# Two attentions: scores and row maxima two groups ahead, turned maxima one group ahead in mid-group

## The reference, cut to what matters

```python
def xattn(query, key, value):           # layer 0; layer 1 is the same with biases and no mask
    q, k, v = split_heads(query @ Wq.T), split_heads(key @ Wk.T), split_heads(value @ Wv.T)
    scores = einsum("bhqd,bhkd->bhqk", q, k) / sqrt(16)
    scores = where(causal | attention_mask, -inf, scores)
    attn = softmax(scores, axis=-1)
    return merge_heads(einsum("bhqk,bhkd->bhqd", attn, v)) @ Wout.T + b_out

x = x + xattn(layernorm(x), ctx, ctx)   # attention 0
x = x + moe_16_experts(layernorm(x))
x = x + xattn(layernorm(x), ctx, ctx)   # attention 1
x = x + moe_7_experts_and_a_shared(layernorm(x))
```

## Time and profile before

| what | us |
| --- | --- |
| runs of the kernel | 1264.04, 1265.51, 1271.85 |
| median | 1265.51 |
| span of the profiled execution | 1262.1 |
| its own time | not listed apart from the three runs |
| a middle batch of attention 0 / its groups | 24.3 / 4 |
| a middle batch of attention 1 / its groups | 23.5 / 4 |

### The profile page before, as it was taken

How to read it: one execution, slowest core, us unless ns; L and a number is a source line. 1 busy time by engine, 2 the same in 40 slices (tenths; PEclk the granted TensorE clock), 3 DMA queues, 4 the chain that set the end, 5 groups by cost and what they waited for, 6 DMA issues and landing times. The chain is left out here.

```text
span 1262.1 us, 25941 instructions
## 1 busy us (share of the span) xinstructions
PE 1123.7 (89%) x8539; PEld 974.6 (77%) x8539; DVE 690.8 (55%) x1558; ACT 595.9 (47%) x1211; POOL 360.7 (29%) x502
## 2 busy tenths in 40 slices
PE   5999998739999984888998679999999999999997
PEld 4788786329888873555665379999999999999996
DVE  4755666652222226676767655555556555555556
ACT  3566666313222222776787334444445444444432
POOL 6566650112222205776630145000000000000261
PEclk8899999859999996999999879999999999999999
DMA  7774461548999957568471221223232232232132
GB/s 182 175 180 120 129 179 37 193 159 292 332 330 325 314 207 163 111 136 146 89 125 24 100 89 59 79 63 112 72 103 76 87 109 87 86 100 73 50 97 80
DMA packets 88137, 172.56 MB, mean 137 GB/s; under 512 B 11251, under 2 KB 59949, under 8 KB 81792
## 3 DMA queue, kind: packets, MB, share of 16 engines
q1 hardware_dynamic: 71712, 136.15, 39.0%
q0 software_dynamic: 9584, 29.32, 7.9%
q10 hardware_dynamic: 6768, 6.16, 1.4%
HBM read 133.11 MB, written 39.20 MB: 137 GB/s over the span
## 5 line engine op out<-in xcount | busy, mean ns | idle before, releaser
L2136 PE MATMUL e_ps<-xT_e,wp_e 128*128 128x384 f32 (+1 forms) x1344 | 245.2, 331 | 4.0 <-DVE wp_e L2010 4.0
L2136 PEld LDWEIGHTS e_ps<-xT_e,wp_e 128*128 128x128 f32 x1344 | 221.7, 188 | 5.4 <-issue 4.1
L639 DVE TENSOR_REDUCE att_ps<-att_ps 128x2 f32<-128x512 f32 (+1 forms) x224 | 155.3, 697 | 103.5 <-PE att_ps L986 63.2
L1968 ACT ACTIVATE act_a_e<-e_ps 128x256 f32<-128x256 f32 (+2 forms) x176 | 77.8, 442 | 159.9 <-PE e_ps L2136 150.9
L2066 DVE TENSOR_TENSOR hid_e<-act_a_e,e_ps 128x256 f32<-128x256 f32 (+2 forms) x176 | 87.0, 494 | 116.6 <-ACT act_a_e L1968 102.4
L892 ACT ACTIVATE probs<-att_ps 128x384 f32<-128x384 f32 (+1 forms) x256 | 130.4, 546 | 41.4 <-PE att_ps L1018 29.0
L1972 ACT ACTIVATE hidp_e<-hid_e 128x256 fp32r<-128x256 f32 (+2 forms) x176 | 83.8, 476 | 127.3 <-DVE hid_e L2066 121.5
L2153 PE MATMUL e_ps<-wp_e,hidp_e 128*128 128x256 f32 (+1 forms) x1008 | 138.4, 282 | 2.9 <-DVE xres L2026 1.2
L2068 DVE TENSOR_TENSOR hidp_e<-hid_e,hidp_e 128x256 fp32r<-128x256 f32 (+2 forms) x176 | 87.8, 499 | 95.5 <-ACT hidp_e L1972 90.1
L2153 PEld LDWEIGHTS e_ps<-wp_e,hidp_e 128*128 128x128 f32 (+1 forms) x1008 | 130.7, 183 | 4.9 <-issue 4.1
L1608 ACT ACTIVATE hid_e<-e_ps,b_ahead 128x128 f32<-128x128 f32 x188 | 53.7, 368 | 139.9 <-PE e_ps L1713 129.2
(11 more groups left out here) (235 smaller groups left out, 1850.0 us busy)
## 6 DMA issues: line engine op xcount, KB each, us to landing
w_e<-in_W SPq DMA_DIRECT2D x47, 1024.0 KB
w_e<-in_W SPq DMA_DIRECT2D x57, 384.0 KB, 3.1
ks<-parts SPq DMA_DIRECT2D x96, 128.0 KB, 4.7
qs<-parts SPq DMA_DIRECT2D x96, 128.0 KB, 5.2
parts<-cut SPq DMA_DIRECT2D x30, 384.0 KB, 3.2
x_e<-rows SPq DMA_DIRECT2D x8, 768.0 KB, 5.6
done<-y_e ACTq DMA_DIRECT2D x47, 128.0 KB
rows<-zeros POOLq DMA_DIRECT2D x8, 736.5 KB, 6.6
```

The source lines that it names most:

```text
L639: dve.tensor_reduce(tops_at(at[3])[:, qt, x0:x0 + heads], src, AX.X, ALU.max).then_inc(reduced, 1)
L1968: act.activation(act_a[:, u % 2, 0:n], ps[:, AB + u % 2, 0:n], ACT.Silu).then_inc(silu_ready, 1)
L2136: last = pe.matmul(ps[:, bank + u % 2, 0:n], weights(lot, c, pw)[:, (b * DC + d) * P:(b * DC + d + 1) * P], xT[:, px, d, t0:t0 + n], start ...
```

## The change

Scores and maxima are computed two groups ahead instead of one (`after(after(at))` on TensorE and VectorE), the turn and the copy of the maxima one group ahead, in the middle of a group: after the second transposed score on TensorE, and after the second exponential on ScalarE. The values of the group before move behind the second transposed score as well, the turn of their output to the group's end. The row maxima are kept in a new SBUF tile `row_tops`, and their turned row in PSUM bank MB, so that the wait on the exponentials before the turn is dropped. A prologue computes the scores, maxima and copied row of the first groups.

```diff
--- before.py
+++ after.py
@@ -184,6 +184,7 @@
         qs, ks = sb("qs", [KT, 2, H, S], BF16), sb("ks", [KT, 2, H, S], BF16)
         stacks = (qs, ks)
         top_parts = sb("top_parts", [P, 2, TPB, 2, G], BF16)
+        row_tops = sb("row_tops", [P, 2, TPB, G])
         probs = sb("probs", [P, 2, G, TPB * S])
         v = sb("v", [P, 2, TPB, H, ROWS])
         o = sb("o", [P, 2, S])
@@ -304,9 +305,13 @@
 
             return bank + f if early(f) else XB
 
+        def turned_tops(lo, hi):
+
+            return ps[KS:KT, MB, lo:hi]
+
         def tops_at(g):
 
-            return ps[:, MB, (g % 2) * TPB * G:(g % 2 + 1) * TPB * G].rearrange("p (t x) -> p t x", t=TPB)
+            return row_tops[:, g % 2]
 
         def comes(n, kind):
 
@@ -695,13 +700,13 @@
                 gathered = ye is not None and normed_ahead(n)
                 for g in range(NG):
                     at = (n, j, r, g)
-                    more, started = not (last and g == NG - 1), not (first and g == 0)
+                    more, started = not (last and g >= NG - 2), not (first and g == 0)
                     for u in range(NU):
                         if g == 0 and u == 0 and gathered:
                             rows_back(dve, f)
                             dve.wait_ge(root_ready, f - 1)
                         if more:
-                            reduce(after(at), u)
+                            reduce(after(after(at)), u)
                         if g == 0 and gathered:
                             t, c = u % TPB, u // TPB
                             if u == TPB:
@@ -722,7 +727,7 @@
                         if g == 3 and u and not first and u <= TPB:
                             statistics(n - 1, u - 1)
                     if more:
-                        tops(after(at))
+                        tops(after(after(at)))
                     if started:
                         normalize(prior(at))
                     if g == 2 and first and ye is None:
@@ -787,11 +792,12 @@
                     dve.wait_ge(later_ready, 1)
                     close(dve, 0)
                 split(dve, 1, 1)
-            for u in range(NU):
-                reduce((0, 0, 0, 0), u)
-            tops((0, 0, 0, 0))
-            if ye is None:
-                split(dve, 1, 0)
+            for g in range(2):
+                for u in range(NU):
+                    reduce((0, 0, 0, g), u)
+                tops((0, 0, 0, g))
+                if ye is None and g == 0:
+                    split(dve, 1, 0)
             batches(dve, batch)
             normalize((B - 1, 1, None, NG - 1))
             residual(B - 1)
@@ -878,12 +884,6 @@
             def batch(n, j, r, first, last):
                 for g in range(NG):
                     at = (n, j, r, g)
-                    act.wait_ge(top_turned, ready(group(at)))
-                    act.activation(qs[KS:KT, j, g * G:(g + 1) * G, :], ps[KS:KT, TB, 0:S].unsqueeze(1).to_broadcast([2 * G, G, S]),
-                                   ACT.Copy).then_inc(row_ready, 1)
-                    if not (first and g == 0):
-                        take(prior(at))
-
                     act.wait_ge(valued, free(group(at)))
                     for x0 in range(G):
                         slot = g * G + x0
@@ -892,6 +892,18 @@
                         act.activation(probs[:, g % 2, x0, 0:WIDE], ps[:, TB + x0 % RING, 0:WIDE], ACT.Exp, scale=DK ** -0.5).then_inc(exped, 1)
                         if slot in H_SLOTS and fed(n):
                             norm_rows(n + FEED, j, H_SLOTS.index(slot))
+                        if x0 == 1:
+                            if not (first and g == 0):
+                                take(prior(at))
+                            if not (last and g == NG - 1):
+                                set_rows(after(at))
+
+            def set_rows(at):
+
+                n, j, r, g = at
+                act.wait_ge(top_turned, ready(group(at)))
+                act.activation(qs[KS:KT, j, g * G:(g + 1) * G, :], turned_tops(0, S).unsqueeze(1).to_broadcast([2 * G, G, S]),
+                               ACT.Copy).then_inc(row_ready, 1)
 
             def square_root(f, n, k):
 
@@ -924,6 +936,7 @@
                     take_values(f)
             if ye is None:
                 act.activation(warm[:], offset[:, 0:1], ACT.Exp)
+            set_rows((0, 0, 0, 0))
             batches(act, batch)
             take((B - 1, 1, None, NG - 1))
             take_all(B - 1)
@@ -992,9 +1005,8 @@
             def turn_tops(at):
                 n, j, r, g = at
                 pe.wait_ge(top_ready, ready(group(at)))
-                pe.wait_ge(exped, free(n * H + g * G))
                 for t in range(TPB):
-                    last = pe.matmul(ps[KS:KT, TB, t * P:(t + 1) * P], top_parts[:, g % 2, t].rearrange("p a g -> p (a g)"),
+                    last = pe.matmul(turned_tops(t * P, (t + 1) * P), top_parts[:, g % 2, t].rearrange("p a g -> p (a g)"),
                                      m["identb"][:], start=True, stop=True, tile_position=(0, KS))
                 last.then_inc(top_turned, 1)
 
@@ -1099,32 +1111,33 @@
             def batch(n, j, r, first, last):
                 for g in range(NG):
                     at = (n, j, r, g)
-                    more, started = not (last and g == NG - 1), not (first and g == 0)
+                    more, started = not (last and g >= NG - 2), not (first and g == 0)
 
                     def score_next(u):
                         if more and u < NU:
-                            score(after(at), u)
+                            score(after(after(at)), u)
 
                     if first and g == NG - 1 and ahead is None:
                         pe.wait_ge(wo_loaded, 16)
                     score_next(0)
-                    turn_tops(at)
-                    if started:
-                        value(prior(at))
-                    score_next(1)
                     scoreT(at, 0)
                     feed(n, j, r, g * G)
                     if ye is not None and first and g == 0:
                         pe.wait_ge(taken[0], FEED)
                     scoreT(at, 1)
+                    if started:
+                        value(prior(at))
+                    score_next(1)
+                    feed(n, j, r, g * G + 1)
+                    if not (last and g == NG - 1):
+                        turn_tops(after(at))
+                    scoreT(at, 2)
                     score_next(2)
-                    feed(n, j, r, g * G + 1)
+                    feed(n, j, r, g * G + 2)
+                    scoreT(at, 3)
+                    score_next(3)
                     if started:
                         turn_o(prior(at))
-                    scoreT(at, 2)
-                    score_next(3)
-                    feed(n, j, r, g * G + 2)
-                    scoreT(at, 3)
                     feed(n, j, r, g * G + 3)
 
             if constants:
@@ -1167,6 +1180,10 @@
                 pe.wait_ge(identb_ready, 1)
             for u in range(0 if ye is None else RING, NU):
                 score((0, 0, 0, 0), u)
+            score((0, 0, 0, 1), 0)
+            turn_tops((0, 0, 0, 0))
+            for u in range(1, NU):
+                score((0, 0, 0, 1), u)
             batches(pe, batch)
             ended = (B - 1, 1, None, NG - 1)
             value(ended)
```

## The result

The changed kernel takes 1323.93 us (median of 4 runs, 1319.71 to 1331.02), the kernel before 1268.13 (1264.04 to 1271.85): ratio 1.0443, interval 1.041 to 1.0477, so it is slower by some 56 us. The forecast was 1288.5 with a range to 1302: the sign is right, but the 23 us forecast are less than half of the 56, and the time lies outside the range. The profiled execution is the longest of the four (1331.02 us), that of before the shortest of its own (1264.04), so stage by stage the traces differ by 67 us and not by 56.

The account below looks back on a forecast made before the run. It took the stack's landing, asked for one group earlier, as the bound: +14.5 us in attention 0 and +8.7 in attention 1, 23 on 1265.5, gave 1288.5 us. Range 1268 to 1302.

Parts of the forecast that it names:

- the stack's landing binds: Both attentions: group 2 now waits for the next batch's stack, 1 to 6 us each, 20 to 35 us in all.
- Rival 1: Whole kernel: not slower, the stack's landing is not the bound; 1253.5 us, or 1249; chance 0.08.
- rival 2: Whole kernel: about no change, stack binds at the quick end and removed waits pay the rest; +9, 1275 us; chance 0.20.
- Landing at 0.6 + 12.5 = 13.1 after the start against 11.75: 1.3 us a batch, and it comes again in every batch: Attention 0, batches 1 to 5: stack wait recurring each batch, 6.5 us in all (bounds 3.5 and 21).
- Batch 6, the last stack: Attention 0, batch 6: landing stays, but two short groups follow it instead of one, +4.3 us.
- The start of attention 0: Attention 0, first batch: a stack wait of 5.6 us including the longer prologue, taken as 5.0 (bounds 1 and 8).
- batch 1 of attention 1: Attention 1, batch 1: landing fixed by GpSimd's split, two groups after it instead of one, +6.2 us.
- Batches 2 to 5: Attention 1: 25.4 us a batch, four 101.6 against 98.6 measured before, +3.0 us (bounds -3 and +10).
- Rival 4, the clock: Whole kernel: new waits lower TensorE's clock, 1.7 us after 8 of 14 stack waits, +14, 1302 us; chance 0.15.
- In attention 0 it cancels the waits removed: Attention 0: turn apart from values costs 0.2 us a group, offset by removed waits of 0.16 a group.
- ScalarE's copy in mid-group at 0: ScalarE's 1.02 us copy behind the second exponential costs 0, covered by TensorE's transposed scores, scores and a turn.
- Maxima in SBUF at 0: VectorE writing maxima to SBUF and two small operations reading it cost 0 (bounds -0.1 and +0.1 us a group).

Follow-up runs that it names:

- after_free: The changed kernel with stack loads of batches 2 to 7 sent to a spare tile, so no score waits for them: 1280.74 us, ratio 1.0093.
- border: The changed kernel, but the next batch's groups 0 and 1 are both scored in the last group, none in group 2: 1294.25 us, ratio 1.0188.
- before_apart: The kernel before, with a unit of full score matmuls put between the turn of the maxima and the values: 1272.44 us, ratio 1.0033.
- free_eased_together: free_eased with the turn of the maxima directly behind the values: 1270.39 us, ratio 1.0024.
- free_eased: after_free with ScalarE's projection taken ahead of the maxima copy and the output's turn back behind the third transposed score: 1277.26 us, ratio 1.0069.
- after_together: The changed kernel with the turn of the maxima directly behind the values: 1329.26 us, ratio 1.046.
- together_fill_last: after_together with GpSimd's zero stores issued behind the last batch of attention 0 instead of one in each batch: 1307.86 us, ratio 1.0309.

## Why the prediction was right and wrong

- **That the stack's landing binds, and that scores two groups ahead ask for it in group 2: right.** The waits stand at L997 in nearly all batches, 32.7 us in all (20 to 35 forecast). `after_free` and `border` each take away the early due time by another way and get 44 and 32 us back. Rival 1 (not slower) and rival 2 (+9) are out.
- **"Landing at 0.6 + 12.5 = 13.1 after the start against 11.75: 1.3 us a batch, and it comes again in every batch": the step that failed.** The term gave 6.5 for batches 1 to 5 of attention 0 and measured 23.3. Three things were missing in it. First, batch 1 isn't a middle batch. Its stack waits for GpSimd's split: the loads start 3.6 us behind the batch's first exponential (69.96 against 66.4), where they started 0.9 behind it before (61.87 against 61.0), since the longer start holds back the split as well; landing then takes 14.4 us, the wait is 6.0 and the clock takes over 2. Second, loads take 12.8 to 15.4 us, not 12.5. The row of 107.39 was the quickest: by the landing events of its trace the kernel before loads the stacks of its batches 1 to 6 in 14.7, 12.0, 11.8, 12.5, 14.2 and 15.4 us. Third, 7.4 of the 23.3 stay when no stack is waited for (`after_free`, 129.0 us for these five batches against 121.6): the forecast took the old 24.3 us for everything but the wait.
  The waits of batches 2 to 5 came out as forecast, 4.8 us against 5.2, but by luck: the loads were longer, and the new order put group 2's first score later, 12.85 us after the batch's first score in `after_free` instead of 11.75. With the 6.0 of batch 1 they make 10.9; the clock, charged nowhere in the term, is about 4 (from landing to the next batch 16.4 and 15.6 us behind the two waits that lowered it, 13.7 and 14.2 in `after_free`).
- **Batch 6, the last stack.** Forecast +4.3 in attention 0, measured +7.8: landing 14.3 us behind the batch's first exponential instead of 12.8 (1.5), and 2.1 of clock. In attention 1 the same term was left out: the sum named batches 1 to 5 and the "last two batches, where nothing is loaded in the second", though stack 7 is loaded in the first of these. Measured +5.5 there, a wait of 4.7 us with its clock.
- **The start of attention 0, and batch 1 of attention 1.** The wait forecast in the first batch (5.0) wasn't one: batch 0 starts 5.3 us later, some 3 by the prologue and 2 by the late first load, and then the next stack is just in time. A right sum by another road, and by luck. Batch 1 of attention 1 (+6.2) had the mechanism, two groups behind a fixed landing; it measured 9.2, and behind the wait of 7.04 us the clock was 0.50 for 4 us. Batches 2 to 5 (+3.0) measured +8.1. The recorded text says that loads start just after a batch begins, "at 613.19 in that of 608.0", but that is 5.2 us; the 0.9 was about right all the same for the changed kernel, whose loads are issued from 0.5 us before to 1.8 behind the first exponential. The bounds of this term, by its own loads of 11.9 and 15, come to -1.4 and +11, not to -3 and +10.
- **Rival 4, the clock, was the nearest one.** It had 8 waits at 1.7 us; there were 6 at 1.7 to 2. Its 1302 still falls 22 us short, since it kept the forecast's other terms. It was held unlikely since "mine are 1.3 to 2.3 in most batches". That is true of most, but two of those (2.25 and 1.66 us) lowered the clock too, and the long ones are just those at the ends, which the forecast itself had put at 4.3 and 6.2 us: no clock term was charged for its own long waits.
- **"In attention 0 it cancels the waits removed": wrong.** The form's price was put somewhat high: `before_apart` and `free_eased_together` show 0.1 to 0.17 us a group for a pair of changes, not 0.2. But the removed waits didn't pay even for that: batches free of the stack rose from 24.3 to 26.0. The rest of that rise is new short waits behind ScalarE's order and the late turn (1.0 us in a middle batch by `free_eased`; the two were not moved apart).
- **ScalarE's copy in mid-group at 0: wrong in attention 0.** The cover named was work of the transposed scores. What was late instead was a projection's bank, taken out behind the copy. It had to be asked which of ScalarE's other work queues up behind the copy, not only what TensorE does meanwhile.
- **Maxima in SBUF at 0 (bounds -0.1 and +0.1 us a group): inside its bounds, wrong in its reason.** VectorE had time to spare; the operations weren't slower but held up by GpSimd, and TensorE stands behind them. Alone, in the old order, it costs 5 to 6 us, 0.09 a group.

## What to carry to other kernels

Running ahead by one more stage asks for everything that the stage reads one stage earlier: before it, look for the transfer whose landing has the least margin to its first reader, at the first and last rounds too, where the rounds are shorter or the producer is late. A wait of TensorE of some 5 us cost about 2 us more through the clock here, and two of five waits of 1 to 2.3 us were followed by a lower clock too. A batch's own length in the new order has to be forecast as well, not taken from the old one. A small operation on a critical chain was better left reading PSUM than moved to SBUF beside a busy GpSimd, even with its engine half idle.

## What the runs showed of the hardware

The same stack loads run at two rates, with the DMA engines busy all the time in both. First 5 us of the kernel before, then 11 us of `after_together` (windows, columns as in rows 2):

```profile
112.00:117.00 5.00, 5.00 (x64) 4.25 (x63) 2.83 (x8) 4.13 (x9) 3.72 (x5) 1.00 1.04 227
```

```profile
133.00:144.00 11.00, 7.46 (x80) 6.11 (x79) 5.85 (x15) 6.18 (x12) 4.77 (x5) 1.00 1.07 143
```

The share is 1.04 and 1.07, the rate 227 and 143 GB/s. Packets of 4 KB take 0.29 us in the one and 0.47 to 0.5 in the other. That GpSimd's zero stores have a part in it is shown by `together_fill_last`, not how: the slow window holds none of their packets. The kernel before has the slower rate too, 0.47 us a packet from 568 to 577 in attention 1; what sets it there stays open. A busy DMA share therefore doesn't say how long a load still takes.

And a VectorE operation of 8 elements a partition can last 2.12 us, just as long as the GpSimd instruction beside it: a group's mean of 431 ns shows it only to those who ask for the longest of the group.
